# The output stage's layernorm epilogue taken for two 128-token tiles at a time

## The reference

```python
x = _layernorm(x + _L0_attn_ref(x, ...), axis=-1)
x = _layernorm(x + _L0_ffn_ref(x, ...), axis=-1)

# in _L0_ffn_ref
logits   = einsum('bnd,des->bnes', x_unit * scale, mu_unit)
dispatch = softmax(logits, axis=1)
combine  = softmax(logits.reshape(B, N, E * S), axis=-1).reshape(B, N, E, S)
slot_in  = einsum('bnd,bnes->besd', xn, dispatch)
h        = gelu(einsum('besd,edh->besh', slot_in, w1) + b1)
slot_out = einsum('besh,ehd->besd', h, w2) + b2
out      = einsum('besd,bnes->bnd', slot_out, combine)
```

## Time and profile before

| | us |
|---|---|
| three runs shown | 5390.22, 5638.33, 5650.19 |
| their median | 5638.33 |
| the profiled execution | 5400.94 |
| span of its slowest core | 5399.3 |
| spans of its 8 cores | 5377.2 to 5399.3 |
| mean granted TensorE clock of a core (share of 2.4 GHz) | 0.767 to 0.771 |

### The profile page before, as it was taken

One profiled execution on the slowest core, in us unless ns is written; L12 is line 12 of the kernel. 1 busy time (PEld: TensorE's weight loads), 2 busy tenths in 40 slices (PEclk: granted clock), 3 DMA queues, 4 the chain that ended last, 5 costly groups with the idle time before them and its releaser, 6 DMA issues.

```text
span 5399.3 us, 38737 instructions; the slowest of 8 cores (5377.2 to 5399.3 us)
## 1 busy us (share of the span) xinstructions
PE 3012.6 (56%) x11945; PEld 1191.1 (22%) x11945; DVE 1219.0 (23%) x1734; ACT 1724.1 (32%) x3086; POOL 182.1 (3%) x315
## 2 busy tenths in 40 slices
PE   0005867676667667676767676667667653411111
PEld 0002323232222222222223222223222221100000
DVE  0000122222121222221222223121222232133333
ACT  0002243333334242524243333434242522222222
POOL 1000000000000000000000000000000000001010
PEclk9999877787778788787878787778778865555555
DMA  9996322222212122222222221312222112322222
GB/s 113 109 124 126 88 71 66 83 68 68 84 53 83 52 85 67 83 68 87 66 69 71 79 83 52 84 52 83 56 85 78 54 31 65 98 76 76 76 77 77
DMA packets 230315, 413.14 MB, mean 77 GB/s; under 512 B 79042, under 2 KB 96466, under 8 KB 226658
## 3 DMA queue, kind: packets, MB, share of 16 engines
q1 hardware_dynamic: 210738, 287.39, 16.8%
q0 software_dynamic: 19376, 123.27, 13.5%
HBM read 352.46 MB, written 101.19 MB: 84 GB/s over the span
## 4 chain that ended last, share of the span: by engine, by line
PE 41%; DVE 19%; ACT 15%; issue 10%; another core or an unknown queue 5%; DMA 4%; SPq 3%; DVEq 1%; POOL 1%; ACTq 1%; POOLq 0%
PE pSA L451 8%; PE pSB L451 8%; DVE st L71 4%; PE pAT L557 3%; ACT jb L71 3%; ACT st L71 3%; DMA exp_in<-expb 3%; DVE slot_in L71 3%; PE pTR L943 3%; PE pOa L672 3%; DVE tA L71 3%; SPq L392 2%; PE pSA L605 2%; DVE tB L71 2%
## 5 line engine op out<-in xcount | busy, mean ns | idle before, releaser
L451 PE MATMUL pSA<-x_fm,wbufA 128*128 128x512 bf16 x1536 | 435.5, 435 | 350.4 <-ACT hbuf L71 176.7
L451 PE MATMUL pSB<-x_fm,wbufA 128*128 128x512 bf16 x1536 | 391.2, 401 | 0.0
L451 PE MATMUL pSA<-hbuf,wbufB 128*128 128x512 bf16 x1024 | 273.6, 415 | 189.9 <-ACT q_fm L71 121.0
L1251 PE MATMUL pTR<-identS,exp_in 128*128 128x128 bf16 x128 | 23.8, 289 | 528.3 <-DMA exp_in<-expb 528.3
L71 ACT ACTIVATE exp_t<-pTR,rl2s 128x256 bf16<-128x256 f32 x64 | 30.3, 473 | 834.1 <-PE pTR L896 834.1
L451 PEld LDWEIGHTS pSA<-x_fm,wbufA 128*128 128x128 bf16 x1536 | 163.4, 108 | 583.4 <-issue 451.0
L943 PE MATMUL pTR<-xn_bf,exp_t 128*128 128x512 bf16 x256 | 145.8, 569 | 226.6 <-DVE slot_in L71 195.0
L451 PE MATMUL pSB<-hbuf,wbufB 128*128 128x512 bf16 x1024 | 260.8, 401 | 0.0
L71 DVE TENSOR_TENSOR tA<-tB,lnw_b 128x2048 f32<-128x2048 f32 x32 | 73.4, 2292 | 699.8 <-ACT tB L71 699.8
L71 DVE TENSOR_TENSOR slot_in<-pTR,slot_in 128x512 f32<-128x512 f32 x256 | 177.2, 692 | 228.9 <-PE pTR L943 228.9
L557 PE MATMUL pAT<-q_fm,k_fm 128*128 128x512 bf16 x512 | 186.0, 529 | 65.2 <-DVE at_s L71 48.7
(11 more groups left out here) (148 smaller groups left out, 4277.9 us busy)
## 6 DMA issues: line engine op xcount, KB each, us to landing
wbufA<-wb SPq DMA_DIRECT2D x48, 2048.0 KB, 10.1
wbufB<-wb SPq DMA_DIRECT2D x48, 2048.0 KB, 10.2
Sbf<-S POOLq DMA_DIRECT2D x16, 2048.0 KB, 12.7
OUT<-out_sb SPq DMA_DIRECT2D x64, 512.0 KB, 3.4
xb<-x POOLq DMA_DIRECT2D x1, 16384.0 KB, 156.2
x_tm<-xb SPq DMA_DIRECT2D x16, 1024.0 KB, 6.8
xprime<-xp_t POOLq DMA_DIRECT2D x64, 256.0 KB, 2.3
xp_in<-xprime POOLq DMA_DIRECT2D x64, 256.0 KB, 2.8
```

The source lines that it names most:

```text
L451: mm = t.matmul(p[:, :], wbuf[:, kc, m * 128:(m + 1) * 128], src[:, kc, :], start=(kc == 0), stop=(kc == NCH - 1))
L1251: mm = t.transpose(pTR[:, ec * 128:(ec + 1) * 128], exp_in[:, par, ec * 128:(ec + 1) * 128], ident[:, :])
```

## The change

The loop takes two tiles at a time. `emit_bEpi` and `emit_bstats` give way to `emit_bEpi_pair(tix)`, for tiles `tix` and `tix + 1`:

- VectorE waits for the matmuls of both tiles, then does sum and row sum for the one and the other.
- ScalarE squares both, and copies four columns of `st8` where it copied two for each tile.
- The columns of `st8` are laid out so that a quantity's values of both tiles are neighbours (`stbp`), and the small operations for mean, mean square, variance, Ln and Exp run once on 128x2. The variance's fused multiplication and subtraction becomes two operations. NMR is made for each tile.
- ScalarE writes both halves of `out_sb`, then SP issues both stores.
- `v_pO_release`, `a_bepi_end` and `v_b_tile` of both tiles are noted at the points of the pair.

The order of emission changes: the epilogue of the pair before is emitted ahead of `emit_bPE(tix)` and `emit_bPE(tix + 1)`. `emit_bPE` itself is the same. The loads of a pair thus wait, both of them, for the end of VectorE's part of the epilogue of the pair before, and the epilogue no longer has the next tile's PE work ahead of it.

```diff
--- before.py
+++ after.py
@@ -1198,32 +1198,10 @@
     a_bepi_end = {}
 
     def stb(par, col):
-        return st8[:, par * 16 + col: par * 16 + col + 1]
-
-    def emit_bstats(par):
-        def fv(v, raw, par=par):
-            W(raw, "v", A)
-            v.tensor_scalar_mul(out=stb(par, MEAN), in0=stb(par, S1), scalar1=INV_C)
-            v.tensor_scalar_mul(out=stb(par, S2C), in0=stb(par, S2), scalar1=INV_C)
-            v.scalar_tensor_tensor(out=stb(par, NVAR), in0=stb(par, MEAN),
-                                   scalar=stb(par, MEAN), in1=stb(par, S2C),
-                                   op0=ALU.mult, op1=ALU.subtract)
-        vector_section(fv)
-
-        def fs(sc, raw, par=par):
-            W(raw, "sc", V)
-            sc.activation(out=stb(par, RSTD), in_=stb(par, NVAR),
-                          func=AF.Ln, scale=-1.0, bias=eps_c[:, 0:1])
-            sc.activation(out=stb(par, RSTD), in_=stb(par, RSTD),
-                          func=AF.Exp, scale=-0.5)
-        scalar_section(fs)
-
-        def fv2(v, raw, par=par):
-            W(raw, "v", A)
-            v.tensor_scalar(out=stb(par, NMR), in0=stb(par, MEAN),
-                            scalar1=stb(par, RSTD), scalar2=-1.0,
-                            op0=ALU.mult, op1=ALU.mult)
-        vector_section(fv2)
+        return st8[:, col * 2 + par: col * 2 + par + 1]
+
+    def stbp(col):
+        return st8[:, col * 2: col * 2 + 2]
 
     v_expT = {}
 
@@ -1274,53 +1252,79 @@
             peO.inc(mm)
         peo_bt[tix] = peO.n
 
-    def emit_bEpi(tix):
-        par = tix % 2
-        pO = pOa if par == 0 else pOb
-
-        def f_bstt(v, raw, tix=tix, pO=pO, par=par):
-            W(raw, "v", peO, peo_bt[tix])
+    def emit_bEpi_pair(tix):
+        def f_bstt(v, raw, tix=tix):
+            W(raw, "v", peO, peo_bt[tix + 1])
             W(raw, "v", A, a_bepi_end.get(tix - 2))
-            v.scalar_tensor_tensor(out=tC[:, par, :], in0=pO[:, :],
-                                   scalar=rcden[:, tix:tix + 1],
-                                   in1=xp_in[:, par, :],
-                                   op0=ALU.mult, op1=ALU.add)
-            v.reduce_sum(out=stb(par, S1), in_=tC[:, par, :], axis=AX.X)
+            for k in range(2):
+                v.scalar_tensor_tensor(out=tC[:, k, :], in0=(pOa if k == 0 else pOb)[:, :],
+                                       scalar=rcden[:, tix + k:tix + k + 1],
+                                       in1=xp_in[:, k, :],
+                                       op0=ALU.mult, op1=ALU.add)
+                v.reduce_sum(out=stb(k, S1), in_=tC[:, k, :], axis=AX.X)
         vector_section(f_bstt)
         v_pO_release[tix] = V.n
-
-        def f_bsq(sc, raw, tix=tix, par=par):
+        v_pO_release[tix + 1] = V.n
+
+        def f_bsq(sc, raw, tix=tix):
             if tix == 0:
                 pin_act(raw, SET_LNEXP)
             W(raw, "sc", V)
-            sc.activation(out=jC[:, :], in_=tC[:, par, :], func=AF.Square,
-                          accum_out=stb(par, S2))
-            sc.activation(out=st8[:, par * 16 + 12: par * 16 + 14],
-                          in_=st8[:, par * 16 + 0: par * 16 + 2], func=AF.Identity)
+            sc.activation(out=jC[:, :], in_=tC[:, 0, :], func=AF.Square,
+                          accum_out=stb(0, S2))
+            sc.activation(out=jC[:, :], in_=tC[:, 1, :], func=AF.Square,
+                          accum_out=stb(1, S2))
+            sc.activation(out=st8[:, 24:28], in_=st8[:, 0:4], func=AF.Identity)
         scalar_section(f_bsq)
 
-        emit_bstats(par)
-
-        def f_bout(sc, raw, par=par):
+        def fv(v, raw):
+            W(raw, "v", A)
+            v.tensor_scalar_mul(out=stbp(MEAN), in0=stbp(S1), scalar1=INV_C)
+            v.tensor_scalar_mul(out=stbp(S2C), in0=stbp(S2), scalar1=INV_C)
+            v.tensor_tensor(out=stbp(10), in0=stbp(MEAN), in1=stbp(MEAN), op=ALU.mult)
+            v.tensor_tensor(out=stbp(NVAR), in0=stbp(10), in1=stbp(S2C), op=ALU.subtract)
+        vector_section(fv)
+
+        def fs(sc, raw):
+            W(raw, "sc", V)
+            sc.activation(out=stbp(RSTD), in_=stbp(NVAR),
+                          func=AF.Ln, scale=-1.0, bias=eps_c[:, 0:1])
+            sc.activation(out=stbp(RSTD), in_=stbp(RSTD), func=AF.Exp, scale=-0.5)
+        scalar_section(fs)
+
+        def fv2(v, raw):
+            W(raw, "v", A)
+            for k in range(2):
+                v.tensor_scalar(out=stb(k, NMR), in0=stb(k, MEAN),
+                                scalar1=stb(k, RSTD), scalar2=-1.0,
+                                op0=ALU.mult, op1=ALU.mult)
+        vector_section(fv2)
+
+        def f_bout(sc, raw):
             W(raw, "sc", V)
             W(raw, "sc", d_out)
-            sc.activation(out=out_sb[:, par, :], in_=tC[:, par, :], func=AF.Identity,
-                          scale=stb(par, RSTD), bias=stb(par, NMR))
+            for k in range(2):
+                sc.activation(out=out_sb[:, k, :], in_=tC[:, k, :], func=AF.Identity,
+                              scale=stb(k, RSTD), bias=stb(k, NMR))
         scalar_section(f_bout)
         a_bepi_end[tix] = A.n
+        a_bepi_end[tix + 1] = A.n
         v_b_tile[tix] = V.n
+        v_b_tile[tix + 1] = V.n
 
         @block.sync
-        def _(s, tix=tix, par=par):
+        def _(s, tix=tix):
             W(s, "s", A)
-            d_out.inc(s.dma_start(out=out_d[tix * 128:(tix + 1) * 128, :],
-                                  in_=out_sb[:, par, :]), 16)
-
-    for tix in range(ntile):
+            for k in range(2):
+                d_out.inc(s.dma_start(out=out_d[(tix + k) * 128:(tix + k + 1) * 128, :],
+                                      in_=out_sb[:, k, :]), 16)
+
+    for tix in range(0, ntile, 2):
+        if tix >= 2:
+            emit_bEpi_pair(tix - 2)
         emit_bPE(tix)
-        if tix >= 1:
-            emit_bEpi(tix - 1)
-    emit_bEpi(ntile - 1)
+        emit_bPE(tix + 1)
+    emit_bEpi_pair(ntile - 2)
 
 
     @block.sync
```

## The result

| | before | after |
|---|---|---|
| profiled execution, us | 5400.94 | 5355.11 |
| lowest of ten runs, us | 5389.49 | 5332.9 |
| median of ten runs, us | 5494.42 | 5349.5 |
| ratio of the undisturbed runs | | 0.9875, interval 0.9819 to 0.993 |

In some executions of either kernel the cores of one die run longer at a lower granted clock; the ratios, and the times given for the experiments, leave these out, the medians of ten don't, and so the medians lie further apart than the kernels do. So the change makes the kernel 1.2% faster, some 60 to 67 us, and both intervals exclude no change.

A forecast was written before the change was run, and what follows sets the result against it. No engine but a serial chain was taken to bound the output stage; start 17.1, 30 periods 613.8 and tail 25.8 gave 656.7 us, 59.1 less, so 5342 us, range 5310 to 5385 (80%), or 5300 to 5600 across run levels.

The forecast's parts named there:

- The sum: Output stage: durations and hand-overs of one pair's serial chain, 20.26 us plus 0.20 jitter, against 22.41 for two old cycles.
- The front: Pair's chain from the first load's issue to the first big add: 9.03 us.
- the first landing: First load issue of a pair to its first transpose: taken as 3.31 us, 3.17 in the stage's first pair.
- The epilogue: Pair's chain from the first big add to the next load issue: 11.23 us.
- Jitter: Allowance per pair for variation and longer landings: 0.20 us, possibly 0.1 or 0.37.
- The stage: Output stage, final layernorm of each 128-token tile: 715.8 us before, forecast at 656.7 us.
- DVE's start after O(t+1): First big add after the second tile's four matmuls: 1.87 us for them plus 0.18, allowing 0.25 both ways.
- Its cover: Second tile's loads land about 4.3 us after first issue, its transpose can't start before 5.95: 1.6 us to spare.
- The rival on the slower side: Bunched stores delay the second tile's exp_in to 9.15 us, lengthening the period 3.2: 39 us slower, 5440; chance 5%.
- its own list of signs: Observations confirming or refuting each step, among them PE clock 0.50; above 0.50 in the stage would make the prediction wrong.
- the rival's mechanism: Denser PE bursts run matmuls at 2.4 GHz, each group of four losing 0.88 us: 5275 us, 2.3% faster; chance 5%.
- within 2%: Outcome class for the whole kernel's time: within 108 us of before, about what measurement can tell from no change; 93%.

The follow-up runs named there:

- e6: The changed kernel itself, unaltered, timed again in five rounds beside the kernel before: ratio 0.9883, interval 0.9849 to 0.9918.
- e2: Against the changed kernel, the first tile's big add waits for its own tile's matmuls alone, not both tiles': 5266.0 us, 0.977 of the kernel before.
- e8: Against the changed kernel, a pair's two stores are issued only after both loads of the next pair have landed: 5335.1 us, ratio 0.9866.
- e1: Against the kernel before, the pair's order of loads and PE work, but each tile keeps its own complete epilogue: profiled execution 5389.78 us.

## Why the prediction was right, and where it was not

**The sum.** Every term was measured in the changed kernel. The front was put at 9.03 us and took 8.99; the first landing was 3.21, between the 3.17 and 3.31 named. The epilogue was put at 11.23 and took 11.29. Jitter was put at 0.20 a pair and came to 0.23 on core 6. The stage was put at 656.7 us and took 657.7 on core 0 and 659.2 on core 6. The forecast of 5342 us, made from the profiled time of the kernel before, compares with 5338.9 for e6; the median of ten, 5349.5, lies higher for the reason given under the table.

**The wait for the matmuls.** The prediction allowed 0.25 us either way for DVE's start after O(t+1), since a modelled end stood behind it: 2.11 was measured where 1.87 + 0.18 was taken. e2 shows that the term is real, and that it is worth 70 us to take it off the chain.

**The second load.** Its cover held: the second transpose waited for PE, never for its load, and e8 shows that the meeting of loads and stores costs nothing that can be measured (4 us of 5335, the intervals overlap). The rival on the slower side didn't come about.

**The clock.** Here the prediction was partly wrong, by its own list of signs too. It took 0.50 for the whole stage, and the stage's mean was 0.53 on core 0 and 0.52 on core 6. On core 6 the window below stood at 0.67, the matmuls of that pair's second tile took 1.43 us instead of 1.87, and the add followed at 4740.65:

```profile
4735.00:4745.00 10.00, 3.88 (x12) 1.28 (x12) 4.62 (x6) 0.00 (x0) 0.00 (x0) 0.67 0.36 134
...
4738.97 1.43 PE L1250 MATMUL pOb<-so_sb,expT 128*128 128x512 bf16 x4 [0.61 <-DVE expT L71]
...
4740.65 1.28 DVE L71 SCALAR_TENSOR_TENSOR tC<-pOa,rcden,xp_in 128x1024 f32<-128x1024 f32 x1 [1.82 <-PE pOb L1250]
```

So the rival's mechanism occurs, but late in a burst and seldom: of the 64 groups of four matmuls, 7 were shorter than 1.82 us on core 6 and 7 on core 0, each time the second tile's, which makes less than 2 us in all on each. In the kernel before there was none on either core. It can also rise too late to help: on core 6 both groups of the pair at 4816 took 1.86 us, and the clock stood high only behind them, while PE did nothing (window):

```profile
4822.20:4826.00 3.80, 0.00 (x0) 0.00 (x0) 3.59 (x3) 0.00 (x0) 0.00 (x0) 0.89 0.00 0
```

The Trainium skill, "TensorE: Matmul & The Clock Gate", part 1, says sustained activity releases the clock; the trace agrees for some bursts of T, O, T, O with short gaps, which the first pair of the earlier trace rows had not shown. That pair was one sample, from core 0. The same profile of the kernel before has this burst on other cores too, and on cores 1, 3 and 5 its second group took 1.52, 1.45 and 1.65 us. Core 3 of the kernel before:

```profile
4676.66 1.45 PE L1272 MATMUL pOb<-so_sb,expT 128*128 128x512 bf16 x4 [0.61 <-DVE expT L71]
```

So the release could have been read before the result, and its late place in the burst with it: no group there gained the 0.88 us that the rival took for every one, nor did any after (the shortest took 1.35).

**From the sum to the chances: the step that failed.** The prediction said that 2% is about what a measurement of this kernel can tell from no change, and put 93% on "within 2%" although its own sum was 59 us with bounds that all lay on the faster side. Two timings gave 0.9875 and 0.9883 with intervals of about half a per cent to either side. A gain of 1.2% is told from none. The sum called for "faster by a little", and the text named it no change that counts. No working is given for the 2% (108 us), and no row stands behind it; the intervals of the two timings show that about 0.5% can be told. The same goes for the wide range of 5300 to 5600. It was drawn around the spread of the three runs shown (5390 to 5650) and held the time without saying much, while the narrow one, 5310 to 5385, was the one that the terms carried. And 5342, read against the median of 5638.33 that stood in the table, looks like a change of 5%: it was made against 5400.94, and only the ratio of like runs can test it.

**What the account left unsaid.** The prediction opened its list with the round of loads that a pair saves. Laid out by parts, its own numbers give the front of two tiles 8.50 before and 9.03 after, half a microsecond worse, and the epilogues 13.54 before and 11.23 after. e1 measured this: no gain from the order (its front took 9.10), all of it from the merged operations.

## What to carry to other kernels

Where no engine is busy for more than a third of a stage, write out one cycle from the timeline and add up starts to starts: the gaps of 0.1 to 0.4 us at each hand-over are terms like the operations. Before sharing a wait between two tiles, look at what the present order hides, since it may cost what the sharing saves; and ask first why the wait is there at all, for releasing the loads when their buffer had been read (one line) gave four times as much. State a small forecast as a ratio to like runs, and take what can be told apart from the interval of repeated timings, not from the spread of all runs. Before a rival is priced from one burst, read the same burst on the other cores of the trace.

## What the runs showed of the hardware

- Small dependent operations cost by their number: one of 0.16 to 0.30 us on 128x1 or 128x2 takes 0.26 to 0.39 from its start to that of the next, and widening it costs next to nothing (two multiplications 0.41 on 128x1 and 0.44 on 128x2; the `st` copy 0.20 on 128x2 and 0.20 on 128x4).
- With twice as much in flight (640 KB of loads and 1 MB of stores) the median landings of exp_in and of a store grew from 2.7 and 3.4 us to 3.3 and 4.5 on the slowest core, and none of it reached the chain; with the stores held back (e8) they were 2.9 and 3.3.
- The granted clock rose inside some pairs' bursts of transposes and matmuls (a second group of 1.35 to 1.81 us instead of 1.87), behind others' (0.89 over 3.8 us in which PE did nothing), and stayed at 0.50 through the rest, with the same instructions in each.
